# One reordering in the sorting stage, the five smoothing steps in one block, the wide layer in one block

## The reference, cut to what matters

```
h = max(layernorm(x), 0);  x = x + gnn0(h, ...)   # gated messages, 4 attention layers
h = max(layernorm(x), 0);  x = x + gnn1(h, ...)   # softmax over the edges of a node
h = max(layernorm(x), 0);  x = x + gnn2(h, ...)   # five smoothing steps
h = max(layernorm(x), 0);  x = x + gnn3(h, ...)   # graph convolutions with a wide layer

# gnn2, five times; w = dinv[row] * dinv[col]
m = segment_sum(w * h[row], col);  h = 0.2 * m + 0.8 * x

# gnn3, the layers around the wide one (C3 = 144, C9 = 432 columns)
h = batchnorm(relu(gcn_conv(h, Wc1, bc1) + te1), g1, be1)
h = batchnorm(relu(gcn_conv(h, Wc2, bc2) + te2), g2, be2)
```

## Time and profile before

| what | value |
| --- | --- |
| median of 3 runs | 6512.73 us (6512.49 to 6529.81) |
| profiled execution, its own time | 6507.9 us |
| its span | 6506.2 us |
| PE, DVE, ACT, POOL busy | 4439.1, 3850.5, 2249.6, 2664.7 us |
| granted TensorE clock, mean | 0.777 |
| sorting | from the start to about 1590 us |
| smoothing steps | 5516 to 5750 us |
| wide layer | 6004 to 6250 us |

### The profile page before, as it was taken

The page is one execution under the profiler, slowest core; times in us unless marked ns, Lnnn a source line. Parts: engine busy times, 40 slices in busy tenths (PEclk is TensorE's granted clock), DMA queues, the critical chain, the costliest instruction groups (busy, mean ns, idle before and its releaser), DMA issues. The chain is left out here.

```text
span 6506.2 us, 186785 instructions
## 1 busy us (share of the span) xinstructions
PE 4439.1 (68%) x79424; PEld 3653.4 (56%) x79424; DVE 3850.5 (59%) x7907; ACT 2249.6 (35%) x7720; POOL 2664.7 (41%) x2702
## 2 busy tenths in 40 slices
PE   6555565662666649975996699489827755968677
PEld 3332333331555538865885688488725733867577
DVE  5544444444899957756775677477647446445144
ACT  2221221110666625543554355345500424000311
POOL 2455455455766616652663466156620520000000
PEclk6666555555899969986997899599958977978587
DMA  8111111122777633423341443243345433000000
GB/s 314 46 48 46 45 47 47 45 50 49 199 198 201 189 115 137 151 84 120 146 150 54 154 153 140 62 148 147 114 48 179 159 116 105 0 7 4 2 2 10
DMA packets 488150, 656.31 MB, mean 101 GB/s; under 512 B 316481, under 2 KB 370373, under 8 KB 484118
## 3 DMA queue, kind: packets, MB, share of 16 engines
q1 hardware_dynamic: 450965, 595.00, 29.0%
q0 software_dynamic: 33856, 48.44, 3.1%
q10 hardware_dynamic: 2496, 0.98, 0.1%
HBM read 464.16 MB, written 180.09 MB: 99 GB/s over the span
## 5 line engine op out<-in xcount | busy, mean ns | idle before, releaser
L299 POOL DMA_INDIRECT edges<-sb_bk_rec,sb_bk_pos x782 | 771.5, 987 | 765.5 <-DVE sb_bk_rec L513 541.2
L1681 ACT ACTIVATE sb_at_val<-banks,sb_at_prob 128x49 f32<-128x49 f32 x3800 | 773.5, 325 | 516.3 <-PE banks L1621 504.3
L1720 DVE TENSOR_REDUCE sb_at_tops<-banks 128x1 f32<-128x512 f32 x1000 | 626.1, 659 | 319.8 <-PE banks L1601 297.1
L1577 PE MATMUL banks<-sb_near,sb_at_hotT_d 128*128 128x49 bf16 x11100 | 619.1, 185 | 128.4 <-DMA sb_at_hotT_d<-rows_dst_t 65.3
L1535 POOL TENSOR_TENSOR sb_at_key<-sb_at_key,sb_at_attr 128x400 f32<-128x400 f32 (+1 forms) x400 | 371.0, 928 | 707.0 <-ACT sb_at_key L1665 616.2
L1579 PE MATMUL banks<-sb_queryp,sb_at_hotT_s 128*128 128x49 bf16 x11400 | 635.1, 186 | 12.7 <-issue 12.2
L1577 PEld LDWEIGHTS banks<-sb_near,sb_at_hotT_d 128*128 128x128 fp8e4 x11100 | 566.7, 97 | 133.5 <-issue 67.0
L1579 PEld LDWEIGHTS banks<-sb_queryp,sb_at_hotT_s 128*128 128x128 fp8e4 x11400 | 565.3, 96 | 15.6 <-issue 15.0
L1598 PE MATMUL banks<-sb_at_hotT_s,sb_off 128*128 128x512 fp8e4 x1000 | 375.0, 375 | 112.5 <-DVE sb_at_tops L1720 111.1
L1542 POOL TENSOR_TENSOR sb_at_val<-sb_at_val 128x490 f32<-128x490 f32 (+1 forms) x400 | 387.1, 968 | 65.4 <-ACT sb_at_val L1681 64.1
L520 DVE TENSOR_SCALAR sb_bk_pre<-banks 37x425 bf16<-37x425 f32 x49 | 29.1, 594 | 638.3 <-remote 599.9
(11 more groups left out here) (676 smaller groups left out, 10961.3 us busy)
## 6 DMA issues: line engine op xcount, KB each, us to landing
sb_at_attr<-attr SPq DMA_DIRECT2D x100, 760.0 KB, 7.2
sb_at_hotT_s<-rows_src_t SPq DMA_DIRECT2D x100, 608.0 KB
sb_at_hot_s<-rows_src SPq DMA_DIRECT2D x100, 608.0 KB
sb_at_hotT_d<-rows_dst_t SPq DMA_DIRECT2D x100, 592.0 KB
edges<-sb_pad SPq DMA_DIRECT2D x95, 460.0 KB
sb_gt_rec<-edges SPq DMA_DIRECT2D x25, 1748.0 KB
sb_we_hotT<-rows_dst_t SPq DMA_DIRECT2D x52, 592.0 KB, 4.1
attr<-sb_gt_rec SPq DMA_DIRECT2D x25, 760.0 KB
```

Source lines behind the costliest of these rows:

```text
L299: pool.indirect_dma_start(list1, bass.IndirectOffsetOnAxis(pos[:, t:t + 1], 0), rec[:, k, j, :], None).then_inc(sent[k], 16)
L1577: pe.matmul(ps[:, 0, H1 * j:H1 * j + H1], where, what, start=(n == 0), stop=(n == 2))
L1681: ins = act.mul(val[:, v % VB, j, 0, :], ps[:, 5, H1 * j:H1 * j + H1], prob[:, i % 2, k:k + 1])
L1720: dve.tensor_reduce(tops[:, i % 2, g:g + 1], ps[:, 3 + x % 2, 0:P * len(RG[g])], AX, ALU.max).then_inc(s_top, 1)
```

## The change

Three edits.

1. In `bucket`, the two `record` calls of an iteration stand right behind `before`, ahead of `pairs` and `ranks`.
2. The five spreads of the smoothing become one stage, `steps`. The rows of step t+1 are split group by group as step t's results are finished, in two buffers, and PE goes from one step's products to the next without a barrier. ACT's parts are now the upper halves of the f32 words (`high`), so that DVE's subtraction does not wait for ACT.
3. The wide layer becomes one stage, `wide_layer`, over its four passes. Weights are loaded one pass ahead into a second buffer, the first pass's during the spread before it. The mean comes from sums that ACT's relu accumulates, ACT squares with the mean as a bias, and scale and shift are folded into Wc2 by a small matmul instead of being applied to 108x3200 values. The first pass writes z, the last writes y: clearing and copying are gone.

```diff
@@ bucket, VectorE
                 if 0 <= x - 1 < NS:
                     before(x - 1)
+                if 0 <= x - RECORD < NS:
+                    record(2 * (x - RECORD))
+                    record(2 * (x - RECORD) + 1)
                 if 0 <= x - RANK < NS:
                     pairs(x - RANK)
                 if 0 <= x - RANK < NS:
                     ranks(x - RANK)
-                if 0 <= x - RECORD < NS:
-                    record(2 * (x - RECORD))
-                    record(2 * (x - RECORD) + 1)
@@ third_part
-        with nc.Fori(0, 5):
-            spread("step", h[:], h[:], start[:])
+        steps(nc, t, ps, C, dinv, many, left, h, tmp, start[:], 5)
+def steps(nc, m, ps, C, dinv, many, left, h, spare, start, count):
+    GROUPS = Spread.ENDS
+    NG, AHEAD, EARLY = len(GROUPS), Spread.AHEAD, 4
...
+            def end(t, n):
+                bs = GROUPS[n]
+                for d in bs:
+                    y = NB * t + d
+                    dve.wait_ge(s_summed, y + 1)
+                    dve.tensor_reduce(h[:, d, :], ps[:, y % AHEAD, 0:3 * H].rearrange("p (k f) -> p f k", f=H), AX, ALU.add
+                                      ).then_inc(s_added, 1)
...
+            for t in range(count):
+                dve.wait_ge(s_last, NG * (t + 1))
+                dve.wait_ge(s_upper, 2 * NG * (t + 1))
+                rarely(t)
+                for n in range(NG):
+                    end(t, n)
+                    if t + 1 < count:
+                        split_rows(t + 1, n)
...
+            for t in range(count):
+                for d in range(AHEAD):
+                    if t:
+                        pe.wait_ge(s_added, NB * t + d - AHEAD + 1)
+                    for n in range(EARLY):
+                        if d == 0:
+                            split_is(t, n)
+                        for s in GROUPS[n]:
+                            product(t, s, d)
+                for n in range(EARLY, NG):
+                    split_is(t, n)
+                    for d in range(AHEAD):
+                        for s in GROUPS[n]:
+                            ins = product(t, s, d)
...
+                with needed(pe, many):
+                    left.products(pe, ps[:, 7, 0:3 * H], rows(t), *of_step[t])
+                for d in range(AHEAD, NB):
+                    pe.wait_ge(s_added, NB * t + d - AHEAD + 1)
+                    for s in range(NB):
+                        ins = product(t, s, d)
+                    ins.then_inc(s_summed, 1)
@@ fourth_part and the wide layer
-        with stage(nc, "clear_z") as (block,):
...
-        with nc.Fori(0, C9 // MC) as j:
...
-        move("keep_z", y[:], z[:])
+        wide_layer(nc, c, t, ps, y[:], wide, z[:], weights, spare)
...
+            def sum_up(j):
+                pe.wait_ge(s_fold, j + 1)
+                pe.matmul(ps[0:MC + 1, 4 + (G_ * (j + 1)) % 2, 0:C3], factors[:], wide.w2[j % 2][0:MC, :], start=True, stop=True
+                          ).then_inc(s_rows, 1)
+                pe.wait_ge(s_taken, j + 1)
+                for q, bs in enumerate(sums):
...
+            for j in range(J):
+                for g in range(1, G_ + 1):
+                    x = G_ * j + g
+                    if x < G_ * J and (g > 1 or j == 0):
+                        turn_in(x)
+                    mix(x - 1)
+                if j + 1 < J:
+                    turn_in(G_ * (j + 1) + 1)
+                sum_up(j)
...
+                    act.activation(junk, hT[:, at:to], ACT.Square, bias=less, accum_out=squares[:, n:n + 1]).then_inc(s_squared, 1)
...
+                link(dve.tensor_reduce(less, total, AX, ALU.add))
+                dve.tensor_scalar(less, less, -1.0 / N, None, ALU.mult).then_inc(s_mean, 1)
...
+                link(dve.tensor_scalar(factors[:, 0:MC], c["ident"][0:MC, 0:MC], var, None, ALU.mult))
+                dve.tensor_scalar(factors[:, MC:MC + 1], less, var, cols[:, 2:3], ALU.mult, ALU.add).then_inc(s_fold, 1)
+                dve.wait_ge(s_rows, j + 1)
+                dve.tensor_copy(wide.w2[j % 2], ps[0:MC + 1, 4 + (G_ * (j + 1)) % 2, 0:C3]).then_inc(s_taken, 1)
```

More of the change, by code:

```diff
@@ L2925, in third_part @@
+def third_part(nc, ps, x, h, tmp, C, dinv, many, left):
     with ExitStack() as ctx:
@@ L2994, in hidden, with wide_layer @@
+def wide_layer(nc, c, m, ps, y, memory, z, wide, spare, eps=1e-5):
+    PER, J = 2, C9 // MC
     groups = [range(b, min(b + PER, NB)) for b in range(0, NB, PER)]
     sums = [range(b, min(b + 3, NB)) for b in range(0, NB, 3)]
-    pieces = [(at, min(512, N - at)) for at in range(0, N, 512)]
+    G_, S_ = len(groups), len(sums)
+    PARTS = [(0, 2048), (2048, N)]
+    PAIRS_OF = 6
     xT = spare[0:FC, 0:4 * PER * P].rearrange("p (h i n) -> p h i n", h=2, i=2)
-    mean, var = m.sb("hid_mean", [MC, 1]), m.sb("hid_var", [MC, 1])
@@ L2999, in hidden @@
[L2999 to L3003, removed]
+    hT, ones = memory[0:MC, 0:NP], memory[96:MC + 1, 0:NP]
+    small = spare[0:MC, 1024 + C3:]
+    total, less, var, squares = small[:, 0:G_], small[:, G_:G_ + 1], small[:, G_ + 1:G_ + 2], small[:, G_ + 2:G_ + 4]
@@ new lines, in wide_layer, with _ @@
+    factors = m.sb("wl_factors", [MC, MC + 1])
+    with stage(nc, "wide_layer", "w0", "w1", "turned", "copied", "mixed", "relu", "step", "mean", "squared", "var", "root", "fold",
+               "summed", "added", "rows", "taken", "ones") as (
+            block, s_w0, s_w1, s_turned, s_copied, s_mixed, s_relu, s_step, s_mean, s_squared, s_var, s_root, s_fold, s_summed,
+            s_added, s_rows, s_taken, s_ones):
+        s_w = (s_w0, s_w1)
+        @block.sync
+        def _(sp):
+            for j in range(1, J):
+                if j >= 2:
+                    sp.wait_ge(s_added, S_ * (j - 1))
+                for dst, src in wide.pairs(j):
+                    sp.dma_start(dst, src).then_inc(s_w[j % 2], 16)
@@ L3019, in mix @@
                 n = len(groups[g]) * P
                 for i in range(2):
-                    ins = pe.matmul(ps[0:MC, 4 + g % 2, 0:n], w1[:, i, :], xT[:, g % 2, i, 0:n], start=(i == 0),
+                    ins = pe.matmul(ps[0:MC, 4 + x % 2, 0:n], wide.w1[j % 2][:, i, :], xT[:, x % 2, i, 0:n], start=(i == 0),
                                     stop=(i == 1))
                 ins.then_inc(s_mixed, 1)
[L3024 to L3036, removed]
+            def sum_up(j):
[4 more added lines that the diff above has]
+                for q, bs in enumerate(sums):
+                    x = S_ * j + q
+                    if x >= 2:
+                        pe.wait_ge(s_added, x - 1)
+                    for n, b in enumerate(bs):
+                        ins = pe.matmul(ps[:, 6 + x % 2, C3 * n:C3 * n + C3], memory[0:MC + 1, P * b:P * b + P], wide.w2[j % 2],
+                                        start=True, stop=True)
+                    ins.then_inc(s_summed, 1)
@@ L3044, in copy_in @@
                 for i in range(2):
[L3045 to L3065, removed]
+                    act.wait_ge(s_turned, x * 2 + i + 1)
+                    act.copy(xT[:, x % 2, i, 0:n], ps[0:FC, 2 * (x % 2) + i, 0:n]).then_inc(s_copied, 1)
@@ new lines, in _ @@
+            act.wait_ge(s_ones, 1)
+            copy_in(0)
+            for j in range(J):
+                for g in range(1, G_ + 1):
+                    x = G_ * j + g
+                    if x < G_ * J and (g > 1 or j == 0) and g < G_:
+                        copy_in(x)
+                    relu(x - 1)
+                if j:
+                    act.wait_ge(s_added, S_ * j)
+                square(j)
+                if j + 1 < J:
+                    copy_in(G_ * (j + 1))
+                    copy_in(G_ * (j + 1) + 1)
@@ L3067, in _ @@
         @block.vector
         def _(dve):
[L3069 to L3073, removed]
-            dve.wait_ge(s_squared, len(pieces))
-            link(dve.tensor_reduce(var[:], squares[:], AX, ALU.add))
-            link(dve.tensor_scalar(var[:], var[:], 1.0 / N, eps, ALU.mult, ALU.add))
@@ L3169, in beside @@
         return Norm(c, ps, Memory(nc, ctx), f"{name}{j}", columns(y[:], j), tmp[:], rows[i], loads(j, names), **relus)
-    def move(name, to, what):
-        with stage(nc, name) as (block,):
-            @block.vector
-            def _(dve):
-                dve.tensor_copy(to, what)
     time_rows(nc, ps, a, te)
     te1, te2 = te[0, 0:C9], te[0, C9:]
+    weights = Wide(m, a, te1, spare, wide)
     layer_norm(nc, "ln3", x[:], h[:], tmp[:], relu=True)
```

186 lines of the change are left out of this document (144 added, 42 removed).

## The result

The changed kernel takes 6161.35 us (median of 4 runs, 6150.16 to 6174.53), the kernel before 6512.61 (4 runs, 6503.54 to 6529.81): ratio 0.9458, 95% interval 0.9431 to 0.9486. That is 351 us less, where 137 were forecast.

| stretch | before | after | difference | forecast |
| --- | --- | --- | --- | --- |
| sorting, start to end | 1589.2 | 1371.9 | -217.3 | -57 |
| smoothing, from the stage ahead to the one behind | 290.7 | 261.4 | -29.3 | -20 |
| wide layer, between its two neighbours | 247.6 | 140.5 | -107.1 | -60 |
| all the rest, untouched | | | +20 | 0 |

What follows compares the result with a forecast made beforehand. No engine was over 68% busy, so each stage had its own limit; GpSimd's scatters and PE's late `ahead` bound the sorting. 6507.9 - 57 (sorting) - 20 (smoothing) - 60 (wide layer) = 6371, given as 6375 us; range 6170 to 6530.

Steps and rivals of the forecast that it cites:

- the circle: Sorting, per set: copy of sums to GpSimd's start 7.73, scatters 20.23, then 2.7 to the next copy, 30.66 us.
- Full gain: Sorting rival: only GpSimd's own loop counts, 25.0 us per set, -237 us, time 6195; chance 0.30.
- The open size is what PE gets done: Sorting step: PE's progress while held up sets the period, 27.7 to 30.7, middle 29.3 us; -57 us in all.
- PE by time: Sorting rival, no gain: PE works by time, the period stays 30.7 us, time 6432; chance 0.15.
- SP's load as the trigger: Sorting rival, slower: PE's trouble starts with SP's first attribute load during scatters; period 34.4, +158 us, time 6590; chance 0.16.
- VectorE holds GpSimd up: Sorting rival: first scatter waits for `pairs` and the ranks' longest operation, 3 us per set, +126 us, time 6500; chance 0.05.
- the chain: Wide layer, last relu to Wc2's products: 7.2 us in place of 13.8, four times, -26 us.
- between passes: Wide layer, products' end to the next pass's first mix: 8.1 us down to 0.1, three times, -24 us.
- at the start: Wide layer, before the first mix: clearing of z and the load stage's barrier go, 12.7 to 5.6 us, -7 us.
- the clock: Wide layer's mix phases: stay at granted 0.50; upper side, two passes at the upper level, 28 us more gain.
- the flag: Smoothing: reading it in the middle of PE's stream costs 1.0 us in each of five steps, +5 us.
- the first split: Smoothing: the first step splits group by group ahead of its first products, 0 to 5 us, taken as +3.

Runs made afterwards that it cites:

- rec_mid: The changed kernel with the sorting's records between pairs and ranks, so GpSimd starts 2.3 us later per set; 5916.13 us, ratio 0.9774 to the kernel before.
- rec_first: The changed kernel with the sorting's records ahead of the copy of sums; 5937.9 us, ratio 0.9813 to the kernel before.
- wide_stall2: The changed kernel with PE made idle (9.9 us each) ahead of the first mix of wide-layer passes 2 to 4; 5978.05 us, ratio 0.9885 to the kernel before.
- after_again: The changed kernel unaltered, run later on another chip; 5928.89 us against 6045.77 for the kernel before, ratio 0.9807.
- rec_only: The kernel before with only the sorting's records moved right behind the copy of sums; 6055.26 us against 6051.94, ratio 1.000.
- hidden_fill: The kernel before with 28 extra PE matmuls after each wide-layer pass's last mix, where PE waited for the scaling; 6039.69 us, ratio 0.9979.

## Why the prediction was wrong

**The sorting, forecast -57, measured -217.** The reading of the circle was right: 7.73 + 20.23 + 2.7 before, 1.92 + 20.65 + 2.76 now, and the case *Full gain* (period 25.0) named it. The step that failed is "The open size is what PE gets done": I took the silence of PE as slow work, of which a rate (3.8 us in 14.8, or 33 rows) could be carried over, and reckoned 2.7 to 5.7 us left at t = 25.0. Nothing was left. The onset was wrong too: I carried it over as 8.1 us behind GpSimd's start, t = 10.1, but in most sets of the changed kernel the first late answer belongs to matmuls at about t = 13, 11 us behind GpSimd's start. That is earlier than the t = 15.8 of before and leaves 19.6 - 13 = 6.6 us of work, which is done in the 12.3 us to the next copy, at twice the rate that I had carried over. What I had weighed against the full gain, that PE is late by itself, was not a backlog of its own. The distance of 2.7 us behind every run, which I noted as speaking for it, was the evidence to follow.

That the end of GpSimd's run releases PE is argued from this distance, which holds in all sets for two starts (7.73 and 1.92 us), and from the second witness. It was not tested where it happens: `rec_mid` and `rec_first` would have moved the start there, and both ran where nothing holds PE up. The chips without a hold-up show that such a run alone is not enough. What in the chip does it, and why only there, stays open.

The other cases: PE by time (period 30.7) and SP's load as the trigger (34) did not come. *VectorE holds GpSimd up*: a scatter beside L541, which reads two tiles of 400 columns, took 1.59 us instead of 0.97, and the run of 16 grew by 0.4 us; those beside `pairs` took 0.97. The prediction said that by the rule of the Trainium skill, "SBUF — State Buffer", section "SBUF: two separate sides", in full, `pairs` would block GpSimd, at 3 us per set with the ranks. That was misread: the rule is on a 2-port fast mode, and `pairs` is a `tensor_reduce`, for which the same page, in "Who interferes with whom", rules such a mode out on this chip. The trace agrees: the 88 scatters that lie mainly beside it take 0.97 us like the rest.

**The wide layer, forecast -60, measured -107.** The idle time went as worked out: -27 for the chain (forecast -26), -24.5 between passes (-24), -8 at the start (-7), -3 at the end (-2). The term that was mis-sized is the clock, taken as 0 with 28 us as its upper side: 46 us here, 29 to 46 over all executions. `wide_stall2` ties it to the idle time ahead of the phases of passes 2 to 4: 30 us of idle time put back made them 27 us longer. Pass 1, which fell from 30.5 to 18.7, has no such test. The size of 46 is in part luck, since the kernel before was profiled with three phases at 0.50, and two of the four later executions of the same code have only two.

**The smoothing, forecast -20, measured -29.** The two costs that I added, +5 for the flag and +3 for the first split, are not there: 21.2 us of idle time and 8.7 us of matmuls at a lower clock are the whole difference (granted 0.94 to 0.97 over each step before, 1.00 from the second step on now).

Of the 351 us, then, 217 are a gain only where PE is held up behind GpSimd's runs; elsewhere the change is worth 117 (`after_again`), or 143 as the sum of its two other edits (51 + 92). The 217 are read from the stretch of the sorting, in which only the first edit changes the program; no run made that edit alone where PE is held up.

## What to carry to other kernels

When an engine's answer always comes at a fixed distance behind another engine's last instruction, take that circle as the bound and ask how early it can start, however the slow engine's own rows look. Idle time of PE in front of f32 matmul phases can cost about twice its length (30 us and 27 more in `wide_stall2`), since the phase behind it may run at half clock. One profile does not tell what level such a phase gets: the same kernel gave 30.5 and 16.6 us for the same phase. And a time taken at one place can hold a stall that is absent at others: an edit with 217 us at one gained 0.0% (0.998 to 1.002) at another.

## What the runs showed that was not expected

Where the first profiles were taken, PE's answers all but stopped during runs of indirect DMAs from GpSimd in two stages (16 scatters or 37 loads, 1.2 to 1.3 us each) and came back 2.7 us behind the scatters and 5.9 to 6.3 us behind the loads; in the later runs, on four chips, nothing of the kind is seen. The kernel before takes 6512 us in the one case and 6046 to 6061 in the other, with 30.65 against 17.65 us per set (`rec_only`). PE stayed at a granted clock of 0.50 through 53 us without any idle time (`hidden_fill`). Scatters that started beside a VectorE operation on two SBUF tiles could take longer, 1.59 us beside L541 and 3.03 beside L609 (2025 columns), where most take 0.97.
